# State tiles in one SBUF ring of six, half of every second C product on GpSimd, 4 KB rows, and a table of side work per engine

## The chip, the cores and the metric

The kernel runs on one core of a Trainium2 chip. The metric is the device time of one execution in microseconds, measured outside the profiler; three executions of the kernel before are given, and one more was profiled. The engines are TensorE (PE; its weight loads are listed as PEld), VectorE (DVE), ScalarE (ACT), GpSimd (POOL) and SyncE (SP), which here issues all the DMAs.

## The reference

The reference is one transformer-like layer over 8 batches of 512 rows by 256 channels in float32. Four parts follow one another, each with a layer norm ahead and a residual add behind: attention over 16 heads with a latent of 32, a feed-forward network with blockwise FP4 quantisation (twice, before and after the third part), and a bidirectional state-space model (Mamba). The change concerns the last one:

```python
    x = x + _L0_attn_a_ref(_layernorm(x, axis=-1), ...)
    x = x + _L0_ffn_ref(_layernorm(x, axis=-1), ...)
    x = x + _L0_attn_b_ref(_layernorm(x, axis=-1), ...)
    x = x + _L0_ffn_ref(_layernorm(x, axis=-1), ...)
...
            dA = jnp.exp(dt[..., None] * A)
            dBu = dt[..., None] * B_ssm[:, :, None, :] * xc[..., None]
            def step(h, inp):
                dAt, dBut, ct = inp
                h = dAt * h + dBut
                y = jnp.einsum('bdn,bn->bd', h, ct)
                return (h, y)
```

There are 512 inner channels, 16 states each, 512 time steps and two directions: a recurrence of 16384 rows of 512 steps for each batch.

## The kernel before, in words

**Units.** One *unit* K is two tiles (e = 0 and 1) of 128 rows by 512 steps: 8 channels by 16 states a tile. A group g (or p) of 8 units is 128 channels of one direction, a batch is 8 groups or 64 units, and the kernel has 512 units. For a unit, SP loads `dt` and `u` = dt * xc with every channel row repeated over 16 states (`spread_dt`, `spread_u`; four DMAs of 256 KB, in rows of 2 KB); ACT makes `exp(dt * A)` into two PSUM banks (`factors`, L1355); GpSimd multiplies `u` by B into one of four `dBu` tiles (`make_dBu`, L1074, 128x1024); DVE runs the recurrence over each tile (`tensor_tensor_scan`, L943), which writes its states over the factors in PSUM, and then multiplies the states by C into the `dBu` tile (L950, the mark `hc`). PE sums over the states of two units with eight matmuls (`state_sum`, L1657) into the bank `YB`, and DVE empties that bank once a group (`make_ycat`, L868). In the last batch alone, from unit 15 on, every second unit is `shared`: its scan of tile 1 writes to SBUF and GpSimd does that tile's C product (`weigh_state`, L1081).

**Side work.** Beside the units of batch b, all engines work through the other parts of its neighbours: `merge` and the second feed-forward network of batch b-1, then latents, attention, first feed-forward network and `prep` (projection, convolution) of batch b+1. These are written as generators, one for each engine, with numbered steps (183, 230 and 65 of them for the first, a middle and the last batch). Engines take their instructions strictly in program order. A table `VISITS` says how many steps each engine takes in each half of a unit; before, all five engines follow the same row of the table. Batches 1 to 6 share one row ("middle").

**Order within a unit, before.** DVE: scan 0, scan 1, side work, C products of both tiles, side work. ACT: side work, then the two factor tiles of the next unit, each of which waits until DVE has read the bank (its product `hc`), then side work. GpSimd: `dBu` of unit K+2, side work. `make_dBu(K)` waits for PE's sum over unit K-4, which shares its tile; `spread_u(K)` waits for `make_dBu(K-2)`, as `rows_u` has two buffers.

## Time and profile before

| | |
|---|---|
| median of 3 runs | 3791.13 us (3790.64 to 3798.03) |
| the profiled execution's own time | 3796.87 us |
| its span in the trace | 3795.1 us |
| mean granted clock of TensorE | 0.871 of full speed |
| DVE busy | 3057.4 us, 81% of the span |
| PE busy (modelled ends) | 2855.8 us, 75% |
| ACT busy | 1991.5 us, 52% |
| GpSimd busy | 1949.1 us, 51% |
| DMA queue of SP | 688.74 MB, 67.3% of 16 engines |

The span is the time between the first and the last instruction of the trace. The units begin at 332 us, a middle batch takes 442 to 443 us, the last scan ends at 3710 us, and the second feed-forward network of the last batch ends the kernel.

### The profile page before, as it was taken

The page shows a single profiled execution, that of the slowest core. Times are in us where ns is not written, and L with a number is a line of the kernel's source. Part 1 is how long each engine was busy: PE and PEld are TensorE (multiplying, and loading weights), DVE is VectorE, ACT ScalarE, POOL GpSimd, SP SyncE. Part 2 cuts the span into 40 slices and gives each one's busy share as a digit, 9 for nine tenths or more (in the row PEclk, how much of TensorE's full clock was granted, in tenths as well). Part 3 has the DMA queues.
Part 4 walks back from the last instruction along what each step waited for, and adds up shares of the span by engine and source line. Part 5 has one row for each costly group of instructions (what it writes and reads, how often), then busy time and mean ns, then how long its engine had stood idle before and what let it go on. Part 6 is the DMA issues. An engine that isn't in the chain of part 4 may idle for free.

```text
span 3795.1 us, 41535 instructions
## 1 busy us (share of the span) xinstructions
PE 2855.8 (75%) x12965; PEld 1467.3 (39%) x12965; DVE 3057.4 (81%) x4262; ACT 1991.5 (52%) x3811; POOL 1949.1 (51%) x1115
## 2 busy tenths in 40 slices
PE   7963877689776987679776897769866797765436
PEld 3631444245423553245442454235532454422103
DVE  5354889797988989788897979888897888979765
ACT  2533665446653575546654466535755466544332
POOL 2014754556545654447545565456544475456671
PEclk9976988899987998799988999879987999887657
DMA  3007885966668665867759666786658677597890
GB/s 94 1 17 209 212 221 159 273 159 179 175 205 240 174 179 152 252 166 193 206 150 272 160 177 175 204 240 175 180 153 247 168 192 208 144 269 209 233 246 19
DMA packets 373277, 691.40 MB, mean 182 GB/s; under 512 B 52157, under 2 KB 63552, under 8 KB 366912
## 3 DMA queue, kind: packets, MB, share of 16 engines
q1 hardware_dynamic: 373056, 688.74, 67.3%
q8 instruction: 104, 1.70, 0.2%
q14 instruction: 117, 0.96, 0.1%
HBM read 603.65 MB, written 84.93 MB: 181 GB/s over the span
## 4 chain that ended last, share of the span: by engine, by line
PE 42%; DVE 27%; ACT 9%; issue 7%; POOL 7%; DMA 6%; SPq 1%; POOLq 0%; ACTq 0%; DVEq 0%
PE banks L1387 22%; DVE banks L943 7%; PE banks L1579 5%; PE banks L1392 5%; POOL sb_arena L1074 4%; DVE sb_arena L950 4%; PE banks L1657 4%; PE banks L1555 3%; ACT banks L1355 3%; ACT sb_arena L1121 2%; DMA sb_arena<-kept_u 2%; PE banks L1427 2%; DVE sb_arena L652 2%; PE banks L1401 2%; DVE sb_arena L847 2%
## 5 line engine op out<-in xcount | busy, mean ns | idle before, releaser
L1074 POOL TENSOR_TENSOR sb_arena<-sb_arena 128x1024 f32<-128x1024 f32 x512 | 1205.6, 2359 | 970.3 <-PE banks L1657 605.5
L943 DVE TENSOR_TENSOR_SCAN banks<-banks,sb_arena 128x512 f32<-128x512 f32 x999 | 1171.4, 1217 | 277.0 <-ACT banks L1355 203.5
L1355 ACT ACTIVATE banks<-sb_arena,sb_neg_a 128x512 f32<-128x512 f32 x1024 | 665.1, 682 | 982.8 <-DVE sb_arena L950 792.0
L1657 PE MATMUL banks<-sb_arena,sb_w_sum 128*32 128x512 f32 x2048 | 336.5, 729 | 461.7 <-DVE sb_arena L950 363.4
L950 DVE TENSOR_TENSOR sb_arena<-banks,sb_arena 128x512 f32<-128x512 f32 x999 | 636.8, 678 | 0.0
L1392 PE MATMUL banks<-sb_ident,sb_arena 128*128 128x128 f32 (+1 forms) x2083 | 358.5, 296 | 364.3 <-POOL sb_arena L984 153.2
L1121 ACT ACTIVATE sb_arena<-banks 128x512 f32<-128x512 f32 (+2 forms) x720 | 360.6, 517 | 510.7 <-PE banks L1392 344.8
L1392 PEld LDWEIGHTS banks<-sb_ident,sb_arena 128*128 128x128 f32 (+1 forms) x2083 | 242.4, 148 | 575.0 <-ACT sb_arena L1121 224.4
L801 DVE TENSOR_REDUCE sb_nmax<-banks 128x1 f32<-128x512 f32 (+3 forms) x352 | 222.7, 635 | 187.0 <-PE banks L1582 186.5
L1387 PE MATMUL banks<-sb_w_gu,sb_arena 128*128 128x352 f32 x1024 | 362.5, 505 | 5.5 <-ACT sb_arena L1121 5.5
L1579 PE MATMUL banks<-sb_arena 128*128 128x384 f32 (+3 forms) x1024 | 361.1, 464 | 4.5 <-POOL sb_arena L1001 4.5
L1657 PEld LDWEIGHTS banks<-sb_arena,sb_w_sum 128*32 128x32 f32 x2048 | 46.0, 117 | 633.1 <-DVE sb_arena L950 443.6
L991 POOL TENSOR_TENSOR sb_arena<-sb_arena,sb_q_s 128x704 f32<-128x704 f32 x64 | 88.7, 1386 | 377.1 <-DVE sb_arena L670 367.5
L1197 ACT ACTIVATE sb_arena<-banks,sb_nmax 128x512 f32<-128x512 f32 (+3 forms) x512 | 266.2, 536 | 26.4 <-DVE sb_nmax L801 25.7
L1387 PEld LDWEIGHTS banks<-sb_w_gu,sb_arena 128*128 128x128 f32 x1024 | 209.0, 212 | 119.9 <-issue 31.5
L1387 PE MATMUL banks<-sb_arena,sb_w_lat 128*128 128x512 f32 x512 | 233.8, 607 | 13.3 <-DVE sb_arena L788 8.2
L1427 PE MATMUL banks<-sb_arena,sb_w_merge 128*128 128x512 f32 x448 | 215.4, 640 | 0.0
L1401 PE MATMUL banks<-sb_identb,sb_zerob 128*128 128x512 bf16 x640 | 215.1, 411 | 0.0
L1387 PE MATMUL banks<-sb_w_down,sb_arena 128*128 128x256 f32 (+1 forms) x768 | 205.1, 412 | 9.6 <-ACT sb_arena L1121 7.8
L1555 PE MATMUL banks<-sb_arena 128*32 128x128 f32 x2560 | 185.9, 280 | 1.9 <-ACT sb_arena L1121 1.9
L1387 PE MATMUL banks<-sb_arena,sb_w_in 128*128 128x512 f32 x256 | 151.0, 725 | 47.8 <-DVE sb_arena L847 46.9
L1579 PEld LDWEIGHTS banks<-sb_arena 128*128 128x128 f32 x1024 | 156.0, 194 | 66.4 <-issue 43.3
(132 smaller groups left out, 4020.9 us busy)
## 6 DMA issues: line engine op xcount, KB each, us to landing
sb_arena<-kept_dt SPq DMA_DIRECT2D x1024, 256.0 KB, 5.2
sb_arena<-kept_u SPq DMA_DIRECT2D x1024, 256.0 KB, 4.6
kept_xc<-sb_arena SPq DMA_DIRECT2D x16, 1024.0 KB, 4.9
kept_z<-sb_arena SPq DMA_DIRECT2D x16, 1024.0 KB, 5.5
sb_arena<-kept_xc SPq DMA_DIRECT2D x64, 256.0 KB, 5.6
kept_dt<-sb_arena SPq DMA_DIRECT2D x64, 256.0 KB, 3.9
kept_u<-sb_arena SPq DMA_DIRECT2D x64, 256.0 KB, 3.9
sb_arena<-kept_z SPq DMA_DIRECT2D x63, 256.0 KB, 5.8
```

The costliest lines, as they stand in the source:

```text
L943: v.tensor_tensor_scan(products if e == 1 and shared(K) else factors, factors, products, 0.0, ALU.mult, ALU.add).then_inc(V.sem, V.mark("s ...
L950: v.tensor_tensor(dBu[K % SLOTS][:, e], psum[:, e], ct[:, gd % 2], ALU.mult).then_inc(V.sem, V.mark("hc", K, e))
L1074: nc.gpsimd.tensor_tensor(dBu[K % SLOTS], rows_u[K % US], bt[:, gd % 2].unsqueeze(1).to_broadcast([P, 2, T]), ALU.mult).then_inc(G.sem, G. ...
L1121: nc.scalar.activation(dst, src, ACT.Copy).then_inc(A.sem, A.mark(*name))
L1355: nc.scalar.activation(psum[:, e], rows_dt[K % RS][:, e], ACT.Exp, scale=neg_a[:, s, m, j:j + 1]).then_inc(A.sem, A.mark("dA", K, e))
L1387: mm = pe.matmul(dst, lhs, rhs, start=(i == 0), stop=(i == len(pairs) - 1))
L1392: mm = pe.transpose(dst, src, ident[0:src.shape[0], 0:src.shape[0]])
L1401: pe.matmul(psum[:, YB], zerob[:, :], identb[:, :].unsqueeze(1).to_broadcast([P, T // P, P]), start=False, stop=False)
L1427: mm = pe.matmul(psum[:, SB[j]], w_merge[:, k, j * P:j * P + P], ycat[:, k], start=(k == 0), stop=(k == 2 * DT - 1))
L1555: mm = pe.matmul(psum[L * r:L * r + L, SB[4], m * P:m * P + P], val[:, at:at + L], prT[:, slot, c * P:c * P + P], start=(k == 0), stop=(k ...
L1579: pe.matmul(psum[:, bank, e * kl:e * kl + kl], qz[:, m, r], lat[1][:, m, 0:kl], start=(e == 0), stop=False)
L1657: mm = pe.matmul(psum[r:r + L, YB], w_sum[:, L * o:L * o + L], dBu[k % SLOTS][:, e], start=(o == 0), stop=(o == QG - 1))
```

## The change

Five things change. (1) `rows_u` (two tiles) and `dBu` (four) become one ring of six `tiles`: `u` is loaded into the tile, GpSimd multiplies it by B in place, the scan writes its states in place, and the C product is in place too. The PSUM bank is then free when the scan has read it. (2) Both tiles of a unit get their C product in one DVE instruction over 1024 columns (`weigh`), one scan later than before; where the unit is shared, DVE does tile 0 alone. (3) Every odd unit is shared, in all batches. (4) `kept_dt` and `kept_u` lie in DRAM so that one DMA of 512 KB with rows of 4 KB loads both tiles; each store of 256 KB becomes four of 64 KB. `spread_u` comes in pairs, behind the sum over the units that held the tiles. (5) Each engine has its own row in `VISITS`, and ACT makes the second factor tile after the side work of the second half.

```diff
-SLOTS, US, RS = 4, 2, 3
+SLOTS, RS = 6, 3
-SHARED = tuple(range(15, NU, 2))
+SHARED = tuple(range(1, NU, 2))
...
     "middle": {
+        "DVE": "01000001021103040061b0833114520520508000142210103001432211301115"
...
         def shared(K):
-            return K >= NK - NU and K % NU in SHARED
+            return K % NU in SHARED
...
             def store_dt(g):
                 sp.wait_ge(G.sem, G.at("dt", g))
-                sp.dma_start(kept_dt[g], dt).then_inc(s_kept_dt, 16)
+                for r in range(QG):
+                    sp.dma_start(blocks_of(kept_dt[g], r), dt[L * r:L * r + L]).then_inc(s_kept_dt, 16)
...
             def spread_u(K):
                 g, q = divmod(K, NQ)
                 if q == 0:
-                    sp.wait_ge(s_kept_u, 16 * (g + 1))
-                if K >= US:
-                    sp.wait_ge(G.sem, G.at("dBu", K - US))
-                for e in range(2):
-                    sp.dma_start(rows_u[K % US][:, e], over_states(kept_u[g], q, e)).then_inc(s_u[K % US], 16)
+                    sp.wait_ge(s_kept_u, 16 * QG * (g + 1))
+                if K >= SLOTS:
+                    sp.wait_ge(E.sem, summed(K - SLOTS))
+                sp.dma_start(tiles[K % SLOTS].rearrange("p e t -> p (e t)"), over_states(kept_u[g], q)
+                             ).then_inc(s_u[K % SLOTS], 16)
...
-                    if K + US + 2 < NK:
-                        spread_u(K + US + 2)
+                    if K >= 2 and K % 2 == 0:
+                        for n in (K - 2 + SLOTS, K - 1 + SLOTS):
+                            if n < NK:
+                                spread_u(n)
...
+            def scan(K, e):
+                factors, states = psum[:, e], tiles[K % SLOTS][:, e]
+                if K // (DT * NQ) % 2 == 1:
+                    factors, states = factors[:, ::-1], states[:, ::-1]
+                if e == 0:
+                    v.wait_ge(G.sem, G.at("dBu", K))
+                v.wait_ge(A.sem, A.at("dA", K, e))
+                v.tensor_tensor_scan(states, factors, states, 0.0, ALU.mult, ALU.add
+                                     ).then_inc(V.sem, V.mark("scan", K, e))
+
+            def weigh(K):
+                gd = K // (DT * NQ)
+                n = 1 if shared(K) else 2
...
+                v.tensor_tensor(tiles[K % SLOTS][:, 0:n], tiles[K % SLOTS][:, 0:n],
+                                ct[:, gd % 2].unsqueeze(1).to_broadcast([P, n, T]), ALU.mult
+                                ).then_inc(V.sem, V.mark("hc", K))
...
+                    scan(K, 0)
+                    if K >= 1:
+                        weigh(K - 1)
                     advance(side, visits[2 * k])
-                    for e in range(1 if shared(K) else 2):
...
-                        v.tensor_tensor(dBu[K % SLOTS][:, e], psum[:, e], ct[:, gd % 2], ALU.mult
-                                        ).then_inc(V.sem, V.mark("hc", K, e))
+                    scan(K, 1)
...
             def make_dBu(K):
-                if K >= SLOTS:
-                    g.wait_ge(E.sem, summed(K - SLOTS))
...
                     if K + 2 < NK:
                         make_dBu(K + 2)
+                    advance(side, visits[2 * k])
                     if shared(K):
                         weigh_state(K)
-                    advance(side, visits[2 * k])
...
             def factors(K, e):
-                if K >= 1 and e == 1 and shared(K - 1):
+                if K >= 1:
                     a.wait_ge(V.sem, V.at("scan", K - 1, e))
-                elif K >= 1:
-                    a.wait_ge(V.sem, V.at("hc", K - 1, e))
...
                     if K + 1 < NK:
                         factors(K + 1, 0)
-                        factors(K + 1, 1)
...
                     advance(side, visits[2 * k + 1])
+                    if K + 1 < NK:
+                        factors(K + 1, 1)
```

How this moves instructions is seen in the program order. DVE before, in a middle batch beside attention (L943 is the scan, L950 the C product, L801 a softmax maximum, L807 a division):

```order
L943 SCALAR_TENSOR_TENSOR banks<-banks,sb_arena 128x512 x2
L801 TENSOR_REDUCE sb_nmax<-banks 128x1
L950 TENSOR_TENSOR sb_arena<-banks,sb_arena 128x512 x2
L943 SCALAR_TENSOR_TENSOR banks<-banks,sb_arena 128x512 x2
L801 TENSOR_REDUCE sb_nmax<-banks 128x1
L950 TENSOR_TENSOR sb_arena<-banks,sb_arena 128x512 x2
L943 SCALAR_TENSOR_TENSOR banks<-banks,sb_arena 128x512 x2
L807 TENSOR_TENSOR sb_arena<-sb_arena,banks 128x512
```

DVE of the changed kernel, beside the same part (L917 is the scan, L926 the C product, L840 the maximum):

```order
L917 SCALAR_TENSOR_TENSOR sb_arena<-banks,sb_arena 128x512
L840 TENSOR_REDUCE sb_nmax<-banks 128x1 x2
L917 SCALAR_TENSOR_TENSOR sb_arena<-banks,sb_arena 128x512
L926 TENSOR_TENSOR sb_arena<-sb_arena 128x512
L840 TENSOR_REDUCE sb_nmax<-banks 128x1 x3
L860 RECIPROCAL sb_einv<-sb_esum 128x16
L917 SCALAR_TENSOR_TENSOR sb_arena<-banks,sb_arena 128x512
L840 TENSOR_REDUCE sb_nmax<-banks 128x1
L917 SCALAR_TENSOR_TENSOR sb_arena<-banks,sb_arena 128x512
L926 TENSOR_TENSOR sb_arena<-sb_arena 128x1024
```

Two products of 512 columns a unit have become one of 1024 or of 512, both of whose inputs now lie in SBUF (`sb_arena<-sb_arena`), directly behind the next unit's first scan, and side work stands between the two scans.

GpSimd before, in the first batch beside the feed-forward network (L1074 is `make_dBu`, L984 and L991 rescale after the quantisation, L1065 makes `u`):

```order
L984 TENSOR_TENSOR sb_arena<-sb_arena,sb_qx_s 128x512 x2
L1074 TENSOR_TENSOR sb_arena<-sb_arena 128x1024
L1065 TENSOR_TENSOR sb_arena<-sb_arena 128x512
L991 TENSOR_TENSOR sb_arena<-sb_arena,sb_q_s 128x704
L1074 TENSOR_TENSOR sb_arena<-sb_arena 128x1024
L991 TENSOR_TENSOR sb_arena<-sb_arena,sb_q_s 128x704
```

GpSimd of the changed kernel at that place (L1119 is `make_dBu`, L1126 `weigh_state`, L1112 makes `u`, L1030 and L1037 rescale):

```order
L1126 TENSOR_TENSOR sb_arena<-sb_arena 128x512
L1112 TENSOR_TENSOR sb_arena<-sb_arena 128x512
L1119 TENSOR_TENSOR sb_arena<-sb_arena 128x1024
L1030 TENSOR_TENSOR sb_arena<-sb_arena,sb_qx_s 128x512 x2
L1119 TENSOR_TENSOR sb_arena<-sb_arena 128x1024
L1126 TENSOR_TENSOR sb_arena<-sb_arena 128x512
L1037 TENSOR_TENSOR sb_arena<-sb_arena,sb_q_s 128x704
```

Every second `make_dBu` is now followed by a `weigh_state`, which waits for that unit's second scan, and everything behind it on GpSimd waits with it.

SP before, at the end of a group (L581 loads dt, L572 loads u, L554 and L558 store them):

```order
L581 DMA sb_arena<-kept_dt 128x1x512 x2
L572 DMA sb_arena<-kept_u 128x1x512 x2
L554 DMA kept_dt<-sb_arena 128x512
L558 DMA kept_u<-sb_arena 128x512
L581 DMA sb_arena<-kept_dt 128x1x512 x2
```

SP of the changed kernel at such a place (L615 and L606 load, L585 and L590 store):

```order
L606 DMA sb_arena<-kept_u 128x1x1024 x2
L615 DMA sb_arena<-kept_dt 128x1x1024
L585 DMA kept_dt<-sb_arena 4x8x512 x4
L590 DMA kept_u<-sb_arena 4x8x512 x4
L615 DMA sb_arena<-kept_dt 128x1x1024
```

The loads are half as many with twice the columns, and each store has become four of a quarter of the rows.

## Rows read from the trace of the kernel before

**Rows 1.** The page: span, and busy time of each engine.
```profile
span 3795.1 us, 41535 instructions
PE 2855.8 (75%) x12965; PEld 1467.3 (39%) x12965; DVE 3057.4 (81%) x4262; ACT 1991.5 (52%) x3811; POOL 1949.1 (51%) x1115
```

**Rows 2.** Busy time by stretch: first batch, a middle batch, late last batch, tail.
```profile
core 0: us, PE busy (x) PEld busy (x) DVE busy (x) ACT busy (x) POOL busy (x), PEclk, DMA share, GB/s
...
332.00:725.00 393.00, 286.66 (x1358) 142.74 (x1359) 340.37 (x456) 227.04 (x444) 228.91 (x127) 0.83 0.79 214
...
1168.00:1610.00 442.00, 348.67 (x1614) 179.85 (x1613) 378.01 (x528) 246.98 (x472) 238.40 (x135) 0.90 0.72 193
...
3500.00:3710.00 210.00, 90.37 (x306) 30.45 (x306) 154.70 (x175) 75.60 (x120) 143.89 (x80) 0.66 0.87 230
3710.00:3795.00 85.00, 59.38 (x196) 36.37 (x192) 42.79 (x78) 20.67 (x30) 10.13 (x9) 0.80 0.02 7
```

**Rows 3.** The chain that ended last, share of the span by engine.
```profile
PE 42%; DVE 27%; ACT 9%; issue 7%; POOL 7%; DMA 6%; SPq 1%; POOLq 0%; ACTq 0%; DVEq 0%
```

**Rows 4.** DVE's longest waits in 1168 to 1610: us, times, longest.
```profile
DVE banks L943 <- ACT banks L1355: 25.4, 30, 7.8
DVE sb_nmax L801 <- PE banks L1582: 19.8, 22, 1.6
```

**Rows 5.** Groups of instructions in 1168 to 1610: busy, mean ns; idle before.
```profile
L943 DVE TENSOR_TENSOR_SCAN banks<-banks,sb_arena 128x512 f32<-128x512 f32 x129 | 151.1, 1217 | 25.7 <-ACT banks L1355 25.4 <-POOL sb_arena L1054 0.3
L950 DVE TENSOR_TENSOR sb_arena<-banks,sb_arena 128x512 f32<-128x512 f32 x128 | 81.5, 679 | 0.0
...
L1074 POOL TENSOR_TENSOR sb_arena<-sb_arena 128x1024 f32<-128x1024 f32 x64 | 150.6, 2356 | 122.7 <-PE banks L1657 79.2 <-DMA sb_arena<-kept_u 39.1 <-DMA sb_arena<-rows_bc 4.2
```

**Rows 6.** Single lines over the kernel: duration ns min/median/max.
```profile
L652 DVE SCALAR_TENSOR_TENSOR sb_arena<-sb_arena,sb_q_r x70: 891/892/2286, 27.7 to 3777.9; 128x704 f32<-128x704 f32 x70
L652 DVE SCALAR_TENSOR_TENSOR sb_arena<-sb_arena,sb_qx_r x32: 691/692/1364, 191.4 to 3739.1; 128x512 f32<-128x512 f32 x32
...
L943 DVE TENSOR_TENSOR_SCAN sb_arena<-banks,sb_arena x25: 1191/1198/1199, 3465.3 to 3709.1; 128x512 f32<-128x512 f32 x25
...
L1081 POOL TENSOR_TENSOR sb_arena<-sb_arena x25: 1258/1265/1602, 3466.6 to 3710.4; 128x512 f32<-128x512 f32 x25
...
L1074 POOL TENSOR_TENSOR sb_arena<-sb_arena x512: 2336/2355/3001, 327.3 to 3704.7; 128x1024 f32<-128x1024 f32 x171
```

**Rows 7.** GpSimd's and DVE's timeline, 1507 to 1510: start us, us.
```profile
1507.19 2.36 POOL L1074 TENSOR_TENSOR sb_arena<-sb_arena 128x1024 f32<-128x1024 f32 x1 [5.45 <-PE banks L1657]
...
1507.59 0.74 DVE L868 SCALAR_TENSOR_TENSOR sb_arena<-sb_arena,sb_d_skip,banks 128x512 f32<-128x512 f32 x1
...
1508.70 0.87 DVE L678 TENSOR_TENSOR sb_moment<-sb_stats 128x4 f32<-128x4 f32 x1
1509.49 0.15 DVE L679 TENSOR_TENSOR sb_moment<-sb_stats 128x4 f32<-128x4 f32 x1
```

**Rows 8.** DVE's waits in 3500 to 3710, late in the last batch.
```profile
DVE banks L943 <- POOL sb_arena L1074: 21.9, 10, 3.5
DVE banks L943 <- ACT banks L1355: 19.1, 23, 3.7
DVE sb_arena L868 <- PE banks L1657: 12.5, 4, 3.6
```

**Rows 9.** The group of `make_dBu` in 3500 to 3710: busy, mean ns; idle before.
```profile
L1074 POOL TENSOR_TENSOR sb_arena<-sb_arena 128x1024 f32<-128x1024 f32 x41 | 96.3, 2352 | 61.6 <-PE banks L1657 43.6 <-DMA sb_arena<-kept_u 14.8 <-DMA sb_arena<-rows_bc 3.2
```

**Rows 10.** DMA: packets, MB, share; issues with KB each and us to landing.
```profile
q1 hardware_dynamic: 373056, 688.74, 67.3%
...
sb_arena<-kept_dt SPq DMA_DIRECT2D x1024, 256.0 KB, 5.2
...
kept_u<-sb_arena SPq DMA_DIRECT2D x64, 256.0 KB, 3.9
```

**Rows 11.** One of SP's own waits, over the whole kernel.
```profile
SPq L572 <- DMA kept_u<-sb_arena: 71.1, 33, 4.8
```

More of the change, by code:

```diff
@@ L163, in pace @@
-def pace(b):
-    visits = VISITS["first" if b == 0 else "last" if b == B - 1 else "middle"]
+    "first": {
+        "PE": "0034000002e01012310140400101131200010201230012010142240001500203"
+              "0022020111300253e01720030602434110300660105200100010000000200000",
+        "DVE": "0100062104601302111203020010520410002010111202103130111112511211"
+               "2012010020212401070561822421631251111021801001000002100002102000",
+        "ACT": "8001500400052201000030270100014030011011011210212311101203240220"
+               "21200200110301530350076a0230046001603204410420101000010100000000",
+        "POOL": "005010033240215101201301204100520000200010210300007700432310c006"
+                "000200011001100241142086010707010612d000002000010000000010010102",
+        "SP": "1053201210000230020h00010320210002200003100400c0000i310020103001"
+              "01m0003000020110214012110020001063009001009330100001001000000000",
+    },
@@ L167, in pace @@
+def pace(engine, b):
+    visits = VISITS["first" if b == 0 else "last" if b == B - 1 else "middle"][engine]
     return [int(n, 36) for n in visits]
@@ L263, in hybrid_block @@
         xcr = area(2, T)
-        rows_u, rows_dt = [area(2, T) for _ in range(US)], [area(2, T) for _ in range(RS)]
+        rows_dt = [area(2, T) for _ in range(RS)]
         bt, ct = area(2, T), area(2, T)
-        dBu = [area(2, T) for _ in range(SLOTS)]
+        tiles = [area(2, T) for _ in range(SLOTS)]
         at_xT = place[0]
@@ L323, in hybrid_block @@
         s_kept_dt, s_kept_u = sem("dt_stored"), sem("u_stored")
-        s_u = [sem(f"u_spread_{i}") for i in range(US)]
+        s_u = [sem(f"u_spread_{i}") for i in range(SLOTS)]
         s_dt = [sem(f"dt_spread_{i}") for i in range(RS)]
@@ L928, in _ @@
             for b in range(B):
-                visits = pace(b)
+                visits = pace("DVE", b)
                 side = beside(b - 1 if b >= 1 else None, b + 1 if b + 1 < B else None)
@@ L954, in _ @@
                     advance(side, visits[2 * k + 1])
+            weigh(NK - 1)
             make_ycat(NG - 1)
```

98 lines of the change are left out of this document (55 added, 43 removed).

## The prediction

> **What bounds the kernel now.** I read the page first: the span is 3795.1 us, and DVE is busy for 81% of it, PE for 75%, ACT and GpSimd for half [rows 1]. PE's ends are modelled, so its 75% is no measure of distance to a limit; the chain that ended last passes through PE for 42% and through DVE for 27% [rows 3], so two in-order engines hand the path to each other. Then the stretches: in a middle batch of 442 us DVE is busy 378.0 us and idle 64, PE busy 348.7, GpSimd 238.4, and the DMA engines 72% [rows 2]. DVE is the nearest to full. Its idle time goes mostly to two waits: 25.4 us for ACT's factors and 19.8 us for PE's attention scores [rows 4]; 19 us are small change. The factor wait comes from the PSUM bank: ACT may fill it only when DVE has multiplied the states out of it. Late in the last batch, where there is little side work, 210 us hold some 42 units, 5.0 us each (41 times `make_dBu` [rows 9]); DVE is busy 154.7, DMA 87% [rows 2], and DVE waits for `make_dBu` 21.9, for factors 19.1, and for PE's sum 12.5 us [rows 8]. The profiled execution took 3796.9 us, 1.8 more than its span and 5.8 above the median of the three runs; the sum below is made against 3796.9.
>
> **Part 1, the C products on DVE.** Before, a middle batch has 128 of them in 81.5 us [rows 5], 0.637 us each where pairs overlap. After, it has 32 of 1024 columns and 32 of 512. With both inputs in SBUF an operation of 512 columns takes 691 ns and one of 704 takes 892 [rows 6], so 1.047 ns a column: 1024 columns are an estimated 691 + 536 = 1227 ns. 32 x (1.227 + 0.691) = 61.4 us, **20.1 us less**. Late in the last batch nothing is gained, as the odd units are shared there already. The bounds: if pairs had not overlapped, the old ones would be 86.9 us and the gain 25.5.
> One rule of the Trainium skill (VectorE: DVE Perf Modes, the section on the TRN2 errata) gives fixed costs of 58 cycles for SBUF sources and 120 for PSUM sources, which would make the new product some 65 ns cheaper than the old at 512 columns; by it the gain would be an estimated 4 us more a batch. The rows say the opposite, 691 against 679 ns [rows 5, 6], and the sum goes by them.
>
> **Part 2, the scans.** The states go to SBUF instead of PSUM: 1198 against 1217 ns [rows 5, 6], so 128 x 0.019 = **2.4 us less** a middle batch. That form already ran 25 times beside a busy GpSimd within 1191 to 1199 ns.
>
> **Part 3, the lock, a new cost.** The old product read one tensor from PSUM; the new one reads both from SBUF. The timeline shows what that means: L678, two SBUF inputs of 4 columns, takes 0.87 us instead of 0.15 because GpSimd's `make_dBu` runs from 1507.19 to 1509.55, and it ends 0.02 us after it; L868, with PSUM among its inputs, ran at its usual 0.74 under the same operation [rows 7]. The same with wider ones: L652 with 704 columns has a median of 892 and a worst of 2286 ns [rows 6]. So each of the 512 new products that finds GpSimd at work waits for the end of that operation. How often? GpSimd's share is 238.4/442 = 0.54 [rows 2]; its 32 added products of 1.265 us [rows 6] make it 279/432 = 0.65. The time left of a running operation is half its length, weighted by length: 150.6 us of 2.36 us ones and 128 us of about 1.35 us ones give 0.95. A product that comes at random waits 0.65 x 0.95 = 0.61 us. Bounds: near 0.1 if GpSimd is done or merely finishing when DVE arrives; 1.25 if each odd unit's product meets a `make_dBu` just begun (2.2) and each even one's seldom (0.3). The program order speaks for some of that: `weigh_state(K)` starts with the end of the scan K,1, a `make_dBu` follows it, and DVE's product comes one scan and any side work after. I take 0.6: 64 x 0.6 = **38.4 us more** a middle batch. GpSimd in turn waits for a running DVE product (its worst `make_dBu` is 3001 against 2355 ns [rows 6]); covered by its 200 idle us in 442, and if that cover were gone it would be 0.65 x up to 1.2 us a unit.
>
> **Part 4, the waits that go.** ACT now needs the end of scan K,e rather than of the product, so factor 0 is made during scan 1 and side work, and factor 1 during the next scan 0 and product (1.2 + 1.2 us, against 0.68 for the factor). Of the 25.4 us [rows 4] I take **20 less**; 5 stay for factors behind exponentials and copies on ACT's queue. What is late next is the attention score (19.8), which the change leaves. And of the 38.4 us at the lock I take **6 back**, where DVE would have waited for PE anyway. The wait's price is not only DVE's: behind a held product stand the next scan and the side work, for which PE and ACT wait. That is within the sum, as all of it is DVE's time.
>
> **Part 5, loads and SP.** Twice 256 KB at 5.2 us to landing [rows 10] become one DMA; packets halve. Two bounds for the DMA engines' 67.3% [rows 10]: the same bytes at the same rate (no change) or a time per packet that stays (near half). DMA is not what DVE waits for, so I count nothing; it is cover for `spread_u` coming later (it waits for PE's sum over K-6, K-5 and not for `make_dBu`), which leaves four units, 4 x 5.0 us in the densest stretch, for 5 us of landing, 4.7 of two `make_dBu` and the sum. The stores are three more issues each.
>
> **Part 6, the tables.** They move side work by a few units on each engine. No row tells whether that adds or takes a wait; from none to the 19.8 us score wait in either direction; I take zero.
>
> **The sum.** Middle batch: -20.1 - 2.4 + 38.4 - 20 - 6 = -10.1 us, six times: -61. First batch, much the same mix (340.4 busy of 393 [rows 2]): -10. Last batch: up to 3500 us -3; after it 42 units with lock +25, factors -19, half of the `make_dBu` wait -11 (ring of six), products 0: -5. Setup (332 us) and tail (85 us) unchanged. Together -79: 3796.9 - 79 = 3718, and against the median of the runs, 5.8 lower, **3712 us**.
>
> **Rivals.**
> *Lock mild* (0.2): GpSimd runs ahead of DVE thanks to the ring of six and the tables, so most products find it idle or just ending, 0.2 us instead of 0.6: 512 x 0.4 = 205 less, of which some 80% is on DVE's path, -164, so about 3550; to 3640 with 0.4. For it: GpSimd's `make_dBu` waited 79.2 us of a batch for PE's sum [rows 5], and that wait is gone. Against: the same freedom lets it start right when DVE wants the lock.
> *Lock dear, slower than before* (0.22): gains without the lock are 48.5 us a middle batch, or 0.76 us for each of 64 products; above that mean the change loses. In phase as the program order suggests (1.1 us), (1.1 - 0.76) x 512 = 174, with 80% on the path +140: about 3930; at 0.9, 3850. For it: all GpSimd time is now a lock, and its share rises to two thirds.
> *Stores and queues coupled* (0.06): the first loads of a group wait for four stores each of dt and u (3.9 us to landing for one before [rows 10], and SP already waits 71.1 us for them [rows 11]). If each of 63 groups loses 3 us more, 3712 + 190 at most, 3760 to 3850 likely: no gain. The Trainium skill (DMA: Bandwidth & Descriptors, on how many engines a transfer takes) says that a transfer is spread over as many engines as divides its slowest dimension; with four blocks there, these stores would take 4 engines and not 16, which is this rival's mechanism; no run here shows it.
> *No net change* (0.07): the lock takes just the gains, mean 0.76 us, 3784 to 3799.
> The forecast itself has 0.45, its own range 3640 to 3780.
> The lock is also the rule against this change in the Trainium skill (SBUF — State Buffer, "Who interferes with whom"): DVE with two SBUF inputs and GpSimd hold the shared ports exclusively, whole instructions long. The trace agrees, by the 0.87 us above.
>
> **Numbers.** Faster by over 0.2% (7.6 us, about what a measurement here can tell from no change): 0.45 + 0.20 = 0.65; within: 0.07; slower: 0.22 + 0.06 = 0.28. Range 3560 to 3860: it leaves out the cheapest half of the mild case and the dearer half of the dear one, together 0.2.
>
> **What would show it.** DVE's scans at 1198 ns; products with minima near 691 and 1227 ns, and means above by the lock's wait: 0.6 us is right, over 0.76 means slower. The wait of L943 for ACT falls from 25.4 us to 5 a batch. GpSimd's share in a middle batch 0.6 or more, and its `make_dBu` mean above 2.36. DMA share under 0.72. Wrong would be: products that seldom meet GpSimd; a DVE that waits for PE's sums, stores or tiles; or factor waits that stay, because ACT is late by its own queue.

## The result, and the profile after

The changed kernel takes 4001.56 us, median of 4 runs (3999.99 to 4006.57); the kernel before, run beside them, 3790.89 us (3787.67 to 3798.03). The ratio is 1.0555, 95% interval 1.0537 to 1.0574: **5.6% slower**, where the prediction said 3712 us, within 3560 to 3860. In every other comparison below, the kernel before has a median between 3790 and 3796 us. One execution each of e14 and e15 was in the slow state and is left out of their medians.

First the page of the changed kernel: span, busy time of each engine, the DMA queue of the loads (packets, MB, share), the chain's shares, and the issues of the big loads (count, KB each, us to landing).

```profile
span 3998.9 us, 40437 instructions
...
PE 2902.8 (73%) x12901; PEld 1479.9 (37%) x12901; DVE 3198.1 (80%) x3775; ACT 1993.3 (50%) x3811; POOL 2427.8 (61%) x1346
...
q1 hardware_dynamic: 225600, 688.68, 68.4%
...
PE 29%; DVE 27%; POOL 15%; DMA 13%; issue 8%; ACT 6%; SPq 2%; POOLq 0%; DVEq 0%; ACTq 0%
...
sb_arena<-kept_dt SPq DMA_DIRECT2D x512, 512.0 KB, 8.3
sb_arena<-kept_u SPq DMA_DIRECT2D x512, 512.0 KB, 6.9
```

DVE is busy 141 us longer than before, though its C products have fewer columns; the span grows by 204. The chain's share of PE falls from 42% to 29%, and GpSimd and DMA rise from 7% and 6% [rows 3] to 15% and 13%: two things that before stood mostly beside the path now lie on it.

Two of the stretches of [rows 2]: the first batch and a middle batch.

```profile
core 0: us, PE busy (x) PEld busy (x) DVE busy (x) ACT busy (x) POOL busy (x), PEclk, DMA share, GB/s
335.00:751.00 416.00, 281.63 (x1324) 139.39 (x1324) 354.18 (x386) 226.27 (x442) 297.68 (x159) 0.80 0.80 201
1222.00:1694.00 472.00, 361.42 (x1606) 183.41 (x1606) 396.84 (x464) 246.61 (x473) 299.50 (x168) 0.87 0.72 181
```

The middle batch is 30 us longer. DVE's busy time in it is 396.8 us. The terms of the prediction gave 378.0 - 20.1 - 2.4 + 38.4 = 393.9: that half is right. Wrong is DVE's idle time: with the forecast length of 432 us it would have been 38, and it is 75. Next, DVE's longest waits in this middle batch (us, times, longest), to set beside [rows 4].

```profile
DVE sb_arena L917 <- ACT banks L1398: 42.5, 13, 6.8
DVE sb_nmax L840 <- PE banks L1626: 12.6, 14, 2.0
```

The factor wait that was to fall from 25.4 to 5 us rose to 42.5. There are fewer of them, 13 instead of 30, and each is 3.3 us long instead of 0.8. That looks less like a bank that comes free a little late than like something late by a whole transfer. The groups over the whole kernel say who is late (busy, mean ns, then idle time before them and what ended it).

```profile
L1119 POOL TENSOR_TENSOR sb_arena<-sb_arena 128x1024 f32<-128x1024 f32 x512 | 1288.3, 2525 | 271.3 <-DMA sb_arena<-kept_u 170.3 <-DMA sb_arena<-rows_bc 100.4
L917 DVE TENSOR_TENSOR_SCAN sb_arena<-banks,sb_arena 128x512 f32<-128x512 f32 x1024 | 1225.2, 1210 | 357.6 <-ACT banks L1398 288.0 <-POOL sb_arena L1119 62.1 <-POOL sb_arena L1101 7.1
L1398 ACT ACTIVATE banks<-sb_arena,sb_neg_a 128x512 f32<-128x512 f32 x1024 | 689.4, 687 | 924.5 <-DVE sb_arena L917 496.4 <-DMA sb_arena<-kept_dt 427.1
```

ACT's factors (L1398) wait 427.1 us for loads of dt. Before, the same wait came to this, beside DVE's for the factors (waits of the whole kernel before):

```profile
DVE banks L943 <- ACT banks L1355: 203.5, 236, 7.8
ACT banks L1355 <- DMA sb_arena<-kept_dt: 190.3, 53, 10.4
```

And the C products, with the two shapes apart (256 each), in the changed kernel:

```profile
L926 DVE TENSOR_TENSOR sb_arena<-sb_arena 128x1024 f32<-128x1024 f32 x256 | 465.3, 1817 | 0.0
L926 DVE TENSOR_TENSOR sb_arena<-sb_arena 128x512 f32<-128x512 f32 x256 | 275.2, 1075 | 0.0
```

Where GpSimd is idle they take 1.20 and 0.66 us. So 256 x 0.62 + 256 x 0.415 = 265 us are spent at the lock, 0.52 us a product, where 0.6 was taken. The timeline late in the last batch shows the lock and a late load side by side (start us, us; in brackets the idle time before and what ended it).

```profile
3778.23 2.34 POOL L1119 TENSOR_TENSOR sb_arena<-sb_arena 128x1024 f32<-128x1024 f32 x1
3778.26 2.86 DVE L926 TENSOR_TENSOR sb_arena<-sb_arena 128x512 f32<-128x512 f32 x1
...
3793.03 1.20 DVE L926 TENSOR_TENSOR sb_arena<-sb_arena 128x1024 f32<-128x1024 f32 x1
...
3798.46 1.30 ACT L1398 ACTIVATE banks<-sb_arena,sb_neg_a 128x512 f32<-128x512 f32 x2 [6.07 <-DMA sb_arena<-kept_dt]
...
3799.25 1.22 DVE L917 TENSOR_TENSOR_SCAN sb_arena<-banks,sb_arena 128x512 f32<-128x512 f32 x1 [3.89 <-ACT banks L1398]
```

At 3778.26 DVE's product of 512 columns begins 0.03 us behind a `make_dBu` and takes 2.86 us instead of 0.66; it ends 0.55 us after GpSimd does. At 3793.03 one of 1024 columns finds GpSimd idle: 1.20. At 3798.46 ACT has stood 6.07 us for dt, and DVE 3.89 us for ACT.

### The profile page after: what moved, and what is told of

Its sections match the earlier page's. It is cut to its first block, busy times and chain, and to the rows that moved or that the text cites. A ratio compares the mean times of both kernels' runs of the same rounds, so it can differ in the third digit from the quotient of the medians.

```text
span 3998.9 us, 40437 instructions
## 1 busy us (share of the span) xinstructions
PE 2902.8 (73%) x12901; PEld 1479.9 (37%) x12901; DVE 3198.1 (80%) x3775; ACT 1993.3 (50%) x3811; POOL 2427.8 (61%) x1346
## 3 DMA queue, kind: packets, MB, share of 16 engines
q1 hardware_dynamic: 225600, 688.68, 68.4%
## 4 chain that ended last, share of the span: by engine, by line
PE 29%; DVE 27%; POOL 15%; DMA 13%; issue 8%; ACT 6%; SPq 2%; POOLq 0%; DVEq 0%; ACTq 0%
PE banks L1431 14%; DVE sb_arena L917 8%; POOL sb_arena L1119 6%; DVE sb_arena L926 5%; DMA sb_arena<-kept_dt 5%; DMA sb_arena<-kept_u 4%; PE banks L1436 4%; PE banks L1623 4%; PE banks L1701 3%; PE banks L1599 2%; DVE sb_arena L886 2%; DMA sb_arena<-kept_z 2%; DMA kept_u<-sb_arena 2%; ACT sb_arena L1166 2%; DVE sb_arena L691 2%
## 5 line engine op out<-in xcount | busy, mean ns | idle before, releaser
L917 DVE TENSOR_TENSOR_SCAN sb_arena<-banks,sb_arena 128x512 f32<-128x512 f32 x1024 | 1225.2, 1210 | 357.6 <-ACT banks L1398 288.0
L1119 POOL TENSOR_TENSOR sb_arena<-sb_arena 128x1024 f32<-128x1024 f32 x512 | 1288.3, 2525 | 271.3 <-DMA sb_arena<-kept_u 170.3
L1398 ACT ACTIVATE banks<-sb_arena,sb_neg_a 128x512 f32<-128x512 f32 x1024 | 689.4, 687 | 924.5 <-DVE sb_arena L917 496.4
L1701 PE MATMUL banks<-sb_arena,sb_w_sum 128*32 128x512 f32 x2048 | 352.7, 766 | 596.0 <-DVE sb_arena L926 389.7
L926 DVE TENSOR_TENSOR sb_arena<-sb_arena 128x1024 f32<-128x1024 f32 (+1 forms) x512 | 740.4, 1446 | 0.0
L1126 POOL TENSOR_TENSOR sb_arena<-sb_arena 128x512 f32<-128x512 f32 x256 | 345.4, 1349 | 466.8 <-DVE sb_arena L917 466.8
L840 DVE TENSOR_REDUCE sb_nmax<-banks 128x1 f32<-128x512 f32 (+3 forms) x352 | 219.6, 632 | 147.8 <-PE banks L1626 147.1
L1431 PE MATMUL banks<-sb_arena,sb_w_lat 128*128 128x512 f32 x512 | 243.2, 625 | 40.6 <-DVE sb_arena L827 30.4
L1037 POOL TENSOR_TENSOR sb_arena<-sb_arena,sb_q_s 128x704 f32<-128x704 f32 x64 | 89.2, 1393 | 301.3 <-DVE sb_arena L709 291.7
L1471 PE MATMUL banks<-sb_arena,sb_w_merge 128*128 128x512 f32 x448 | 207.0, 618 | 0.0
L1445 PE MATMUL banks<-sb_identb,sb_zerob 128*128 128x512 bf16 x576 | 199.4, 431 | 0.0
```

Of the source, the lines that this page charges most:

```text
L917: v.tensor_tensor_scan(states, factors, states, 0.0, ALU.mult, ALU.add).then_inc(V.sem, V.mark("scan", K, e))
L926: v.tensor_tensor(tiles[K % SLOTS][:, 0:n], tiles[K % SLOTS][:, 0:n], ct[:, gd % 2].unsqueeze(1).to_broadcast([P, n, T]), ALU.mult).then_i ...
L1119: nc.gpsimd.tensor_tensor(tiles[K % SLOTS], tiles[K % SLOTS], bt[:, gd % 2].unsqueeze(1).to_broadcast([P, 2, T]), ALU.mult).then_inc(G.sem ...
L1126: nc.gpsimd.tensor_tensor(tiles[K % SLOTS][:, 1], tiles[K % SLOTS][:, 1], ct[:, gd % 2], ALU.mult).then_inc(G.sem, G.mark("hc", K))
L1398: nc.scalar.activation(psum[:, e], rows_dt[K % RS][:, e], ACT.Exp, scale=neg_a[:, s, m, j:j + 1]).then_inc(A.sem, A.mark("dA", K, e))
L1431: mm = pe.matmul(dst, lhs, rhs, start=(i == 0), stop=(i == len(pairs) - 1))
```

## The experiments

Two theories stood against each other. *The lock*: 265 us of DVE's time is more than the 204 that the span grew by. *The loads*: one DMA of 512 KB lands later than two of 256 KB, and four stores a tensor hold up SP's queue, so that dt comes late. Each run gives its median against the kernel before, with the 95% interval of the ratio. "Less" and "more" are differences of medians. The experiments were run in four groups, each with the kernel before beside it. By the intervals of the two ratios, a difference between two experiments is uncertain by some 10 to 15 us.

**e1_no_lock.** DVE's product by C is replaced by a maximum over an axis of length one: one SBUF input instead of two, over the same columns. The kernel then leaves C out of DVE's share of the states. The operation takes 926 ns in the mean.

```diff
-                v.tensor_tensor(tiles[K % SLOTS][:, 0:n], tiles[K % SLOTS][:, 0:n],
-                                ct[:, gd % 2].unsqueeze(1).to_broadcast([P, n, T]), ALU.mult
-                                ).then_inc(V.sem, V.mark("hc", K))
+                both = tiles[K % SLOTS][:, 0:n].rearrange("p e t -> p (e t)")
+                v.tensor_reduce(both, both.unsqueeze(2), AX.X, ALU.max).then_inc(V.sem, V.mark("hc", K))
```

> The changed kernel, with DVE's C product replaced by a maximum over an axis of length one over the same columns, in place: one SBUF tensor, as many columns, and C is left out of DVE's share of the states. Theory lock (the products' waits for GpSimd are DVE's time and on its path): the line's mean falls from 1446 to some 930 ns, 264 us of DVE time go, and the kernel falls from 4001 to 3740-3800 us. Theory late loads (dt tiles land late, DVE then waits for ACT's factors whatever its own pace): the waits move, ACT's wait for dt grows, and the kernel stays above 3920 us. If both cost, between these.

**e2_old_rows.** Part 4 undone: `kept_dt` and `kept_u` in rows of 2 KB, and for a unit's dt, as for its `u`, two loads of 256 KB; one store.

```diff
-                for r in range(QG):
-                    sp.dma_start(blocks_of(kept_dt[g], r), dt[L * r:L * r + L]).then_inc(s_kept_dt, 16)
+                sp.dma_start(kept_dt[g], dt).then_inc(s_kept_dt, 16)
...
-                sp.dma_start(rows_dt[K % RS].rearrange("p e t -> p (e t)"), over_states(kept_dt[g], q)
-                             ).then_inc(s_dt[K % RS], 16)
+                for e in range(2):
+                    sp.dma_start(rows_dt[K % RS][:, e], over_states(kept_dt[g], q, e)).then_inc(s_dt[K % RS], 16)
```

> The changed kernel with rows of 2 KB: two DMAs of 256 KB for each load, one of 256 KB for each store. Theory late loads by size (one DMA of 512 KB lands after 8.3 us where two of 256 KB landed after 5.2 each; four stores on a few engines): landing falls to 5-6 us, ACT's wait for dt from 427 to some 250 us, the kernel to 3900-3950 us. Theory late loads by SP's order (dt stands behind pairs of u loads that wait for PE's sum): no more than 20 us. Theory lock: within 10 us of the changed kernel.

**e3_one_table.** The changed kernel with the one row a batch of `VISITS` of the kernel before, for all engines.

```diff
-    visits = VISITS["first" if b == 0 else "last" if b == B - 1 else "middle"][engine]
+    visits = VISITS["first" if b == 0 else "last" if b == B - 1 else "middle"]
```

> The changed kernel with the one table of before for all engines. Theory tables (the new rows place side work badly for this chip): 3850 us or less. Theory that the tables were fitted to the new order of the units: 4020-4080 us, slower than the changed kernel. I lean to the second by some 30 us.

**e4_shared_last.** Part 3 undone: units are shared in the last batch alone, there from the first odd unit on.

```diff
-            return K % NU in SHARED
+            return K >= NK - NU and K % NU in SHARED
```

> The changed kernel, with GpSimd taking half of a C product in the last batch alone: elsewhere DVE does 1024 columns for every unit. Theory lock: DVE gains back 224 x 0.53 us = 119 us of work, but GpSimd is locked 290 us less and its products are not waited for: 3960-4020 us. Theory coupling (GpSimd's share of the product delays PE's sum, and so SP's u loads and the dt loads behind them; PE waits 473 us for it): clearly faster, 3900-3950 us.

Measured: e1 3916.0 us, ratio 1.0335 (1.0320 to 1.0351), 86 us less than the changed kernel. e2 3891.64 us, 1.0274 (1.0244 to 1.0304), 110 less. e3 4320.34 us, 1.1388 (1.1362 to 1.1414), 319 more. e4 4044.59 us, 1.0669 (1.0648 to 1.0690), 43 more. So neither theory had it alone, and neither alone brings the kernel back. In e1 the lock's time is gone from DVE, and has partly become another wait (page, and waits of the whole kernel):

```profile
PE 2881.2 (74%) x12901; PEld 1480.9 (38%) x12901; DVE 2936.7 (75%) x3775; ACT 1989.7 (51%) x3811; POOL 2235.1 (57%) x1346
```
```profile
ACT banks L1397 <- DMA sb_arena<-kept_dt: 497.9, 151, 13.0
DVE sb_arena L917 <- ACT banks L1397: 426.3, 166, 8.1
```

DVE is busy 261 us less and GpSimd 193 less (each had stood for the other), but DVE now waits 426.3 us for factors instead of 288.0, and ACT 497.9 for dt. In e2, its page and its waits:

```profile
sb_arena<-kept_dt SPq DMA_DIRECT2D x1024, 256.0 KB, 5.7
```
```profile
ACT banks L1397 <- DMA sb_arena<-kept_dt: 262.0, 81, 10.3
DVE sb_arena L916 <- ACT banks L1397: 197.4, 90, 8.0
```

dt lands in 5.7 us instead of 8.3, ACT waits 165 us less for it, and DVE 91 us less for ACT. e3 shows that the order of the side work is no detail. What waits there, over the whole kernel:

```profile
POOL sb_arena L1096 <- DVE sb_arena L887: 867.9, 178, 20.7
PE banks L1671 <- DVE sb_arena L896: 793.7, 187, 46.5
```

L1096 is `weigh_state`, L887 the scan, L1671 the sum and L896 the product: side work stands between them in places that suited the old order. e4 shows that sharing pays in the changed kernel: without it DVE has a product of 1024 columns in nearly every unit, at 1718 ns in the mean over all products.

```profile
L926 DVE TENSOR_TENSOR sb_arena<-sb_arena 128x1024 f32<-128x1024 f32 (+1 forms) x512 | 879.6, 1718 | 0.0
```

**e5_no_lock_old_rows.** Both at once, e1's edit on e2. **e6_split_loads**: loads of 256 KB again, in rows of 2 KB, the layout and the four stores kept. **e7_u_singly**: `spread_u` one at a time, each behind the sum that it needs.

```diff
-                return kept[q].rearrange("c e t -> c (e t)").unsqueeze(0).to_broadcast([DS, CT, 2 * T])
+                return kept[q, :, e].unsqueeze(0).to_broadcast([DS, CT, T])
...
-                sp.dma_start(rows_dt[K % RS].rearrange("p e t -> p (e t)"), over_states(kept_dt[g], q)
-                             ).then_inc(s_dt[K % RS], 16)
+                for e in range(2):
+                    sp.dma_start(rows_dt[K % RS][:, e], over_states(kept_dt[g], q, e)).then_inc(s_dt[K % RS], 16)
```
```diff
-                    if K >= 2 and K % 2 == 0:
-                        for n in (K - 2 + SLOTS, K - 1 + SLOTS):
-                            if n < NK:
-                                spread_u(n)
+                    if K >= 2 and K - 2 + SLOTS < NK:
+                        spread_u(K - 2 + SLOTS)
```

> Both undone in the changed kernel: rows of 2 KB, and DVE's C product replaced by the one-tensor maximum (C is left out of DVE's share). Alone they gave 86 and 110 us. If each hides the other (with late loads, the time won at the lock is spent waiting for factors, which rose from 288 to 426 us): more than the sum, 3650-3750 us. If they only add: 3800-3820 us. If both are the same path: 3880 us.

> The changed kernel with its layout in DRAM and its four stores, but each load as two DMAs of 256 KB with rows of 2 KB. If the loads' size or row costs the 110 us of the old rows: 3890-3910 us, landing of dt 5-6 us. If the four stores cost them (few engines, late first loads of a group): 3980-4005 us. If half each: 3940.

> The changed kernel, in which SP issues one u load in every unit and not two in every second. If the bursts of 1 MB of u ahead of a dt load make it late: landing of dt falls from 8.3 to some 7 us, ACT's wait for dt from 427 to some 330, the kernel to 3930-3970 us. If not: 3995-4015 us.

Measured: e5 3739.99 us, 0.9852 (0.9829 to 0.9876); e6 3934.5 us, 1.0357 (1.0334 to 1.0380); e7 3970.57 us, 1.0459 (1.0435 to 1.0483). Apart, the two edits of e5 gave 86 and 110 us, together 262: each hides part of the other, as a DVE held at the lock does not miss the factors that come late, and the reverse. With the old rows the lock is worth 152 us (160 by the ratios), 58% of the 263 us that DVE spends at it in e2. e6 splits part 4: 67 us are the loads and 43 the stores (75 and 31 by the ratios). e7 is 31 us faster than the changed kernel, but not as its forecast had it: ACT's wait for dt did not fall to 330 us, it is 437.8. The page of e5, and its waits:

```profile
PE 2851.4 (76%) x12901; PEld 1463.0 (39%) x12901; DVE 2929.1 (78%) x3775; ACT 1990.3 (53%) x3811; POOL 2234.5 (60%) x1346
```
```profile
DVE sb_arena L916 <- ACT banks L1396: 277.6, 129, 8.1
DVE sb_nmax L839 <- PE banks L1624: 166.6, 160, 7.3
ACT banks L1396 <- DMA sb_arena<-kept_dt: 296.0, 91, 10.4
```

It is the most telling run. With no lock and no slow load, the states in SBUF, the shared products and the tables give 56 us against the kernel before (a ratio of 0.9852), where the prediction's 48.5 us a middle batch come to 291 over the six middle batches alone. DVE is busy 128 us less than before, but its span is only 60 us shorter, so 68 of them turned into waiting. Its wait for factors is 277.6 us, against 203.5 before; that for attention scores, 166.6, has not grown (186.5 before).

**e8_before_4kb.** Part 4 alone, put on the kernel before. **e9_before_shared**: part 3 alone on it. **e10_old_rows_u_singly**: e7's edit on e2.

```diff
-SHARED = tuple(range(15, NU, 2))
+SHARED = tuple(range(1, NU, 2))
...
-            return K >= NK - NU and K % NU in SHARED
+            return K % NU in SHARED
```

> The kernel before with the rows of 4 KB and the four stores alone. If part 4 costs by itself what its removal gave (110 us): 3890-3910 us. If the kernel before has slack for loads (two u buffers asked early, dt not behind waits for PE): 3790-3830 us.

> The kernel before, with every odd unit shared in all batches (part 3 alone): the scan of tile 1 writes to SBUF, GpSimd multiplies it by C, and DVE's products all keep their PSUM input, so that they never meet the lock. DVE loses 231 products of 0.64 us = 148 us of work. If DVE's work is the path: 3680-3720 us. If the side chain through PE and the waits for factors hold it (as in the changed kernel without lock and with old rows, where 128 us less DVE work gave 51): 3740-3770 us. If GpSimd's products delay PE's sums: 3800 us or more.

> The changed kernel with rows of 2 KB and one u load in every unit. With rows of 4 KB the single u loads gave 31 us. If the burst matters in bytes: again some 30, 3860 us. If 2 KB rows already took its cost (two loads interleave with the next ones): 3880-3895 us.

Measured: e8 3908.53 us, 1.0293 (1.0271 to 1.0316), +113 us; e9 3917.32 us, 1.0333 (1.0310 to 1.0356), +123; e10 3889.1 us, 1.0259 (1.0219 to 1.0299), within its interval of e2. So part 4 (rows of 4 KB and four stores) costs about the same in the old order, whose products keep an input in PSUM, as in the new; the waits of e8 have the same face:

```profile
ACT banks L1360 <- DMA sb_arena<-kept_dt: 367.8, 89, 13.5
DVE banks L948 <- ACT banks L1360: 277.0, 241, 7.9
```

e10 shows nothing of e7's 31 us once the loads are short. e9 was the surprise: DVE is busy 96 us less than before and the kernel is 123 us slower. Its page and its waits:

```profile
PE 2870.9 (73%) x12965; PEld 1466.4 (37%) x12965; DVE 2961.6 (76%) x4031; ACT 1994.7 (51%) x3811; POOL 2238.3 (57%) x1346
```
```profile
PE banks L1657 <- POOL sb_arena L1081: 385.8, 86, 38.0
POOL sb_arena L1081 <- DVE sb_arena L943: 244.1, 81, 17.4
DVE sb_nmax L801 <- PE banks L1582: 237.8, 202, 7.1
```

The sum's idle time before (first) and in e9, by what ended it:

```profile
L1657 PE MATMUL banks<-sb_arena,sb_w_sum 128*32 128x512 f32 x2048 | 336.5, 729 | 461.7 <-DVE sb_arena L950 363.4 <-POOL sb_arena L1081 97.4 <-issue 0.2
L1657 PE MATMUL banks<-sb_arena,sb_w_sum 128*32 128x512 f32 x2048 | 349.5, 757 | 578.9 <-POOL sb_arena L1081 385.8 <-DVE sb_arena L950 125.7 <-DVE banks L943 64.9
```

GpSimd's product waits for DVE's scan, and PE's sum for that product. The sum's wait for GpSimd rises by 288 us, but its wait for DVE's product falls by 238; in all its idle time grows by 117. On DVE four waits grow: for attention scores (186.5 to 237.8 us), for `make_dBu` (70.4 to 118.1), for factors (203.5 to 232.4) and for the sum (15.3 to 42.5). So a `make_dBu` that stands behind GpSimd's product on its queue is a second candidate beside PE's sum. The last five runs tried to find what a mended version would need.

**e11_old_rows_singly_halves** (on e10) and **e12_before_shared_halves** (on e9): each half of a dt tile has its own semaphore, so that ACT starts with the first.

```diff
-                if e == 0:
-                    a.wait_ge(s_dt[K % RS], 32 * (K // RS + 1))
+                a.wait_ge(s_dt[K % RS][e], 16 * (K // RS + 1))
```

> The same, and the two dt tiles of a unit have semaphores of their own: factor 0 waits for its own 256 KB, and each half is asked for when its factor has been made. ACT waited 262 us for dt with the old rows, DVE 197 us for factors. If late dt is what is left: 30 to 60 us less than with single u loads alone, 3810-3830 us. If the lock is (152 us with old rows) and dt only stood in its shade: under 15 us.

> The kernel before with odd units shared and the dt halves with semaphores of their own: a candidate to beat both kernels. ACT waits 190 us there for dt, DVE 204 for factors, most of it for the bank and not for dt: 10-30 us less than with the shared units alone, 3660-3750 us. At worst the same as these.

**e13_old_rows_psum_tile0** (on e2): scan 0 writes to PSUM as before, and its product, now from PSUM, stands right behind it; tile 1 stays in SBUF.

```diff
+                to = factors if e == 0 else states
...
-            def weigh(K):
+            def weigh(K, e):
...
+                v.tensor_tensor(tiles[K % SLOTS][:, e], psum[:, 0] if e == 0 else tiles[K % SLOTS][:, 1],
+                                ct[:, gd % 2], ALU.mult).then_inc(V.sem, V.mark("hc", K, e))
...
-                    a.wait_ge(V.sem, V.at("scan", K - 1, e))
+                    a.wait_ge(V.sem, V.at("hc", K - 1, 0) if e == 0 else V.at("scan", K - 1, 1))
```

> The changed kernel with rows of 2 KB, in which tile 0 of each unit is scanned into PSUM and multiplied from there directly behind its scan, complete results. 512 of DVE's products (tile 0) then have a PSUM input and cannot meet the lock, 256 (tile 1 of even units) still can. The replacement without any lock gave 152 us. Theory lock: DVE's lock waits fall from some 264 us to 90-130, and the kernel from 3892 to 3780-3820 us. If the waits for factors (the bank is now free one product later) eat it: 3850-3890.

**e14_old_rows_four_stores** (on e2): each store is four of 64 KB, into the old layout. **e15_before_shared_later** (on e9): `weigh_state` stands behind GpSimd's side work of the half unit, as in the changed kernel.

```diff
-                sp.dma_start(kept_dt[g], dt).then_inc(s_kept_dt, 16)
+                for r in range(QG):
+                    sp.dma_start(kept_dt[g, L * r:L * r + L], dt[L * r:L * r + L]).then_inc(s_kept_dt, 16)
```
```diff
+                    advance(side, visits[2 * k])
                     if shared(K):
                         weigh_state(K)
-                    advance(side, visits[2 * k])
```

> The changed kernel with rows of 2 KB, whose stores are four DMAs of 32 rows each to a plain layout, where the slowest dimension has 32 steps and not 4. The split loads with the changed layout were at 3934, plain loads and one store at 3892. If the number of store DMAs costs these 43 us: 3920-3940 us. If the blocked destination (4 by 8 rows) does: 3885-3900 us.

> The kernel before with every odd unit shared, and GpSimd's product behind the unit's first side work, as in the changed kernel. Sharing alone made the kernel before 123 us slower, though DVE had 96 us less to do. If that comes from GpSimd's side work standing behind a product that waits for the scan: 3800 us or less. If from PE's sum that waits for GpSimd's product: 3910 us or more.

Measured: e11 3892.66 us, 1.0266 (1.0230 to 1.0303), and e12 3919.85 us, 1.0336 (1.0304 to 1.0368): nothing, against e10 and e9. For e11 that was the second of its forecasts; e12 missed its 3660 to 3750, which had counted on sharing to gain. e13 3892.23 us, 1.0253 (1.0220 to 1.0285): nothing against e2, though the lock did shrink. The groups of its profiled execution, which was its fastest (3864.57 us):

```profile
L917 DVE TENSOR_TENSOR_SCAN banks<-banks,sb_arena 128x512 f32<-128x512 f32 x512 | 622.8, 1216 | 199.3 <-ACT banks L1396 147.5 <-POOL sb_arena L1117 49.8 <-POOL sb_arena L1099 1.5
...
L925 DVE TENSOR_TENSOR sb_arena<-banks,sb_arena 128x512 f32<-128x512 f32 x512 | 350.3, 684 | 10.3 <-DVE banks L917 0.5
L925 DVE TENSOR_TENSOR sb_arena<-sb_arena 128x512 f32<-128x512 f32 x256 | 330.0, 1289 | 0.0
```

In one kernel, the products with a PSUM input run at 684 ns and those with two SBUF inputs at 1289, against 0.66 free: 256 x 0.63 = 161 us of lock, some 100 less than in e2. These products are the same instruction in one kernel, so it is the second SBUF input that meets the lock, which e1, whose operation is another, could not tell. But tile 0's bank is free only after the product again. Over both tiles DVE waits 243 us for factors, against 197 in e2, and this order also has one product more to start in each unshared unit; the table, made for the other order, stays. e14 3915.71 us, 1.0332 (1.0307 to 1.0357): the number of stores alone costs 24 of their 43 us, and whether their layout costs the rest is within the noise. e15 3924.3 us, 1.0341 (1.0321 to 1.0360): as e9, so the later place of `weigh_state` costs nothing that can be measured and gives nothing.

## Why the prediction was wrong

**The size of the lock was right, and its mechanism.** 0.52 us a product against 0.6 taken; minima of 0.66 and 1.20 against estimates of 0.69 and 1.23; a middle batch of DVE busy for 396.8 us against 393.9. The rule of the Trainium skill that was weighed (VectorE: DVE Perf Modes, the TRN2 errata), an estimated 65 ns less with SBUF sources, has its direction here and not its size: with no GpSimd operation beside them, the products of 512 columns took 664 ns in the mean with two SBUF inputs (43 in the changed kernel) and 680 with one in PSUM (169 in e13). The rows of other operations that the sum went by instead (691 against 679) pointed the wrong way. Scans came to 1210 ns, not 1198, some 1.5 us a batch. GpSimd's share in the middle batch is 299.5/472 = 0.63 (0.65 taken) and its `make_dBu` mean 2525 ns (over 2356 [rows 5]), as "what would show it" said. The 0.87 us of [rows 7] was set against the 0.15 of L679; L678 itself has a median of 0.226, which changes nothing in the reading. The rival *lock dear* has the right sign but not by its mechanism: it needed 0.76 us. (That figure counts the 6 us handed back from the lock among the gains without it; without them the change breaks even at 42.5/64 = 0.66 us, still above the 0.52 measured.)

**Part 4 of the working failed: "Of the 25.4 us I take 20 less".** The wait for factors rose to 42.5 us a batch. It was laid to the bank that DVE frees late. But a wait is put down to the event that came last, and others stood behind the bank: ACT waited 190.3 us for dt in the kernel before already, in few long waits, a row that the prediction never looked at. Even with the lock and the slow loads gone (e5), DVE waits 277.6 us for factors, and ACT 296.0 for dt. What ACT was at while DVE stood idle for factors can be counted from the traces (by instruction, so that the sums come within a tenth of the rows above):

| DVE's waits for factors, us | before | changed | e5 |
|---|---|---|---|
| ACT stood for dt | 32 | 121 | 79 |
| ACT did other work | 62 | 80 | 107 |
| ACT made factors | 86 | 68 | 71 |
| ACT stood for PE | 6 | 19 | 22 |

So freeing the bank earlier moved the wait to dt and to ACT's own queue.

**Part 5 failed: "DMA is not what DVE waits for, so I count nothing".** It costs 113 us on the kernel before (e8) and 110 us here (e2): 67 by the loads, 43 by the stores (e6), 24 of these by their number alone (e14), each uncertain by some 10 to 15 us. The path is dt's: three tiles of dt, the DMA issued when ACT has read the tile, and nothing used until all 512 KB have landed, 8.3 us instead of 5.2 [rows 10]. With short loads, taking each half as it lands gave nothing (e11). SP's own waits at the loads of u and of dt, in the kernel before (first two) and in the changed one:

```profile
SPq L572 <- POOL sb_arena L1074: 975.4, 343, 12.0
SPq L581 <- ACT banks L1355: 307.8, 153, 8.2
SPq L606 <- PE banks L1701: 825.2, 151, 23.2
SPq L615 <- ACT banks L1398: 653.9, 222, 8.3
```

SP takes its loads strictly in program order, so that a dt can stand behind a u that is not yet wanted. That was so before as well, in more but shorter waits; what grew is the longest wait at u, from 12.0 to 23.2 us, and the time at dt. How much of the 110 us comes from landing and how much from dt standing behind a held u was not separated further; e7, which unpairs u, gave 31 us with long loads and none with short ones (e10). A fourth dt tile, the direct test, was not tried. The rival *stores and queues coupled*, at a chance of 0.06, came nearest, but its 3760 to 3850 us lie on both sides of the kernel before and even its 3712 + 190 fall short of 4001.56; it left out the loads, the larger half. Its sign, SP's wait for stored u, did rise from 71.1 us [rows 11] to 168.3, but in e6, with the same four stores and short loads, it is 88.3, and in e14 39.4: it went with the long loads. Whether the stores take 4 engines, its mechanism, was not measured.

**Part 6 failed: tables at zero.** They are worth 319 us to the new order (e3), against at most 19.8 us a batch in the working. That the order's own price eats most of this gain is argued from e5, which keeps both and gains 56 us; no run has the new order with the old table and without the lock and the long loads. Part 3 of the change has the same face: in the changed kernel, with tables made for it, sharing saves 43 us (e4); put alone on the old order and tables it costs 123 (e9). Whether PE's sum waiting for GpSimd's product carries those 123 us, or a late `make_dBu` does, is argued from the waits, not isolated; placing the product later (e15) did not matter, and placing it earlier was not tried.

**And the step beneath all: DVE's busy time was priced as the path.** In e5, 128 us less of DVE's work brought 56; in e9, 96 less brought 123 the other way; in e13, about 100 us less lock (63 us less of DVE's busy time than in e2) brought nothing. The working had a 27% DVE share of the chain before it [rows 3] and still charged DVE's time at 80 to 100%. Taken together: from e5's 3740 us, the lock adds 152 (e2), and part 4 a further 110, which leads to the changed kernel's 4002. So the lock and part 4 make the kernel slower than before, and parts 4 and 6 of the working, with DVE's time priced too high, are, as argued above, why there was so little to set against them. PE's busy time follows (2851.4 in e5, 2855.8 before, 2902.8 in the changed kernel). The granted clock is 0.87 against 0.90 in the middle batch, and 0.850 against 0.871 over the kernel; e5, which is the fastest, has 0.863. What the clock adds is inside the figures above and was not separated.

## What to carry to other kernels

Before a freed buffer is credited with a wait, look at what its waiter waits for next: here ACT's 190 us for dt and its own queue stood behind the bank. A load in a short ring has a latency to pay, not only a rate: merging two 256 KB loads into one of 512 KB moved the same bytes, with the DMA engines busy for 68.4% of the span instead of 62.9% (e6), and cost 67 us. And when in-order engines hand the path to each other, do not price work taken off the busiest at its length: here it brought 33% of it (e1), 44% (e5), 58% (e2 to e5), nothing (e13) or a loss (e9). A new order without its own placement of side work cost 319 us: test each part alone, since they hid and hurt one another here (86 + 110 apart, 262 together).

## What the runs showed of the hardware

A row of 4 KB moved no faster than two of 2 KB. From the page, the busy time of 16 engines over the packets is 16 x 3795.1 x 0.673 / 373056 = 0.110 us a packet of 1846 bytes in the mean before [rows 10], and 16 x 3998.9 x 0.684 / 225600 = 0.194 us for 3053 bytes after: 16.9 against 15.7 bytes a ns. The packets take longer in step with their size, or a little more. e6, the changed kernel with short loads, has 16 x 3933.1 x 0.629 / 373056 = 0.106 us a packet, 17.4 bytes a ns.

The lock holds through more than one operation. Over the whole kernel L926 has this spread (min, median and max in ns):

```profile
L926 DVE TENSOR_TENSOR sb_arena<-sb_arena x512: 658/1200/5611, 338.4 to 3917.7; 128x1024 f32<-128x1024 f32 x86, 128x512 f32<-128x512 f32 x85
```

Around that longest one, GpSimd and DVE ran so (start us, us):

```profile
1374.14 2.52 POOL L1047 TENSOR_TENSOR sb_arena<-sb_arena 128x512 f32<-128x512 f32 x2
1374.43 5.61 DVE L926 TENSOR_TENSOR sb_arena<-sb_arena 128x1024 f32<-128x1024 f32 x1
1376.61 2.35 POOL L1119 TENSOR_TENSOR sb_arena<-sb_arena 128x1024 f32<-128x1024 f32 x1
```

Three GpSimd operations follow each other without a gap, until 1378.96. The product, which began 0.29 us behind the first, ends at 1380.04, 1.08 us after the last of them: it did not get in between. A reduction with one SBUF input (e1) ran at 926 ns in the mean beside the same GpSimd, the time of its columns alone.
